# Second cross attention with eight biased exponentials a tile on ACT, a later load of the last experts' weights, and new orders of work

## The reference

```python
q = (x @ W_q).reshape(b, n, HEADS, DIM_HEAD)          # 8 heads of 64
k = (context @ W_k).reshape(b, j, HEADS, DIM_HEAD)    # 64 keys
v = (context @ W_v).reshape(b, j, HEADS, DIM_HEAD)
sim = jnp.einsum('bihd,bjhd->bhij', q, k) * scale     # scale = 1/8
sim = jnp.where(mask[:, None, None, :], sim, max_neg)
attn = jax.nn.softmax(sim, axis=-1)
out = jnp.einsum('bhij,bjhd->bihd', attn, v).reshape(b, n, INNER)
return out @ W_o + b_o
```

## Time and profile before

| | us |
|---|---|
| median of 3 runs | 253.36 (253.21 to 253.58) |
| the profiled execution | 253.86 |
| its span, first to last instruction | 252.1 |
| PE busy | 231.0 |
| DVE busy | 172.7 |
| ACT busy | 142.3 |
| POOL busy | 78.9 |

### The profile page before, as it was taken

How to read it: one execution, slowest core, us unless ns; L and a number is a source line. 1 busy time by engine, 2 the same in 40 slices (tenths; PEclk the granted TensorE clock), 3 DMA queues, 4 the chain that set the end, 5 groups by cost and what they waited for, 6 DMA issues and landing times.

```text
span 252.1 us, 5538 instructions
## 1 busy us (share of the span) xinstructions
PE 231.0 (92%) x2018; PEld 157.2 (62%) x2018; DVE 172.7 (68%) x574; ACT 142.3 (56%) x297; POOL 78.9 (31%) x137
## 2 busy tenths in 40 slices
PE   8997899878999999999997886899798999999995
PEld 8646577653544766565674543497677575579765
DVE  4472899855858823745236999778655888778995
ACT  0746698953244768765764366675565635434360
POOL 4898900010110565448583131182411000000000
PEclk9999999999999999999999999999999999999999
DMA  4888970494000000000000000000000000000002
GB/s 133 179 184 246 299 178 3 144 314 136 4 0 0 3 3 0 1 0 3 0 1 0 3 1 3 0 3 5 1 3 1 3 0 0 0 4 0 0 3 83
DMA packets 22343, 12.23 MB, mean 49 GB/s; under 512 B 11320, under 2 KB 21309, under 8 KB 22317
## 3 DMA queue, kind: packets, MB, share of 16 engines
q1 hardware_dynamic: 21277, 11.53, 16.7%
q0 software_dynamic: 80, 0.20, 0.8%
q10 hardware_dynamic: 960, 0.16, 0.4%
HBM read 8.74 MB, written 3.15 MB: 47 GB/s over the span
## 4 chain that ended last, share of the span: by engine, by line
PE 36%; DVE 12%; POOL 2%; ACT 2%; issue 1%; DVEq 0%
PE bank L1047 11%; PE bank L1059 10%; PE bank L930 2%; PE bank L1032 2%; PE bank L911 2%; DVE stats L1805 2%; PE bank L969 2%; PE bank L898 1%; PE bank L1005 1%; PE bank L1019 1%; DVE sm L2029 1%; DVE XN L2005 1%; DVE XN L1827 1%; PE bank L1086 1%; POOL Es L537 1%
## 5 line engine op out<-in xcount | busy, mean ns | idle before, releaser
L448 POOL TENSOR_TENSOR rs<-rs,halves 128x4 f32<-128x4 f32 x14 | 14.3, 1022 | 79.7 <-DVE rs L1820 63.8
L524 POOL TENSOR_TENSOR X<-X,att 128x128 f32<-128x128 f32 x72 | 30.6, 462 | 13.1 <-ACT att L1512 13.1
L1047 PE MATMUL bank<-XT,Wb 128*128 128x512 f32 x64 | 29.6, 597 | 0.0
L1980 DVE SCALAR_TENSOR_TENSOR att<-bank,cols,att 128x512 f32<-128x512 f32 x18 | 13.5, 750 | 22.6 <-ACT att L1501 16.6
L1059 PE MATMUL bank<-Wb,att 128*128 128x128 f32 x224 | 27.4, 278 | 0.0
L1059 PEld LDWEIGHTS bank<-Wb,att 128*128 128x128 f32 x224 | 25.9, 192 | 1.5 <-issue 0.8
L1552 ACT ACTIVATE att<-bank 128x512 f32<-128x512 f32 x32 | 18.0, 601 | 8.4 <-PE bank L1047 8.1
L1512 ACT ACTIVATE att<-bank,comb 128x128 f32<-128x128 f32 x72 | 20.2, 380 | 4.1 <-PE bank L930 4.0
L930 PEld LDWEIGHTS bank<-W2a,att 128*128 128x128 f32 x144 | 18.2, 191 | 6.3 <-issue 4.3
L1501 ACT ACTIVATE att<-bank,cols 128x512 f32<-128x512 f32 x18 | 12.6, 697 | 12.8 <-DVE att L1980 7.4
L1560 ACT ACTIVATE big<-bank 128x512 f32<-128x512 f32 x14 | 8.4, 597 | 18.9 <-PE bank L1059 18.9
(11 more groups left out here) (229 smaller groups left out, 469.3 us busy)
## 6 DMA issues: line engine op xcount, KB each, us to landing
o_scratch<-big SPq DMA_DIRECT2D x2, 512.0 KB, 4.0
Wb<-in_L_ffn_W SPq DMA_DIRECT2D x1, 1024.0 KB, 5.3
Wb<-in_L_ffn_W SPq DMA_DIRECT2D x8, 128.0 KB, 5.0
X<-in_x SPq DMA_DIRECT2D x2, 256.0 KB, 3.2
k_scratch<-QKVT SPq DMA_DIRECT2D x1, 512.0 KB, 3.9
q_scratch<-QKVT SPq DMA_DIRECT2D x1, 512.0 KB, 5.1
Wb<-k_scratch SPq DMA_DIRECT2D x1, 512.0 KB, 4.6
v_scratch<-QKVT SPq DMA_DIRECT2D x1, 512.0 KB, 7.0
```

The costliest lines, as they stand in the source:

```text
L448: nc.gpsimd.tensor_tensor(rs[:, 0, cut], rs[:, 1, cut], halves[:, :], ALU.pow).then_inc(l_root[h], 1)
L524: nc.gpsimd.tensor_tensor(X[:, h * HT + t, :], X[:, h * HT + t, :], part0[:, i % 2, t, :], ALU.add).then_inc(f_acc, 1)
L1047: mm(bank[i % 4][:, :], W1b[:, e, f * P:(f + 1) * P], XT[:, half(h)], start=True, stop=True).then_inc(m_up, 1)
```

## The change

The second cross attention no longer subtracts the maximum on DVE. DVE writes the negated maximum (`negative_max1`); ACT scales the queries as it copies them, takes one exponential for each of the eight heads straight from PSUM with the negated maximum as a bias for each partition, and writes each head's sum with it; DVE takes the reciprocal (`inverse_sums1`). The scores' banks are free, for `scores1(t + 2)` and for the next transposes, once the exponentials are through (c_exp instead of c_sub). W1b and W2b are issued behind the second half of `o_scratch` instead of the first. The lists of PE, ACT, DVE and POOL are reordered in many places; the diff below keeps the functions and the moves that the text names.

```diff
@@ sync
-                if h == 0:
+                if h == 1:
                     sp.wait_ge(a_scores, NU)
                     sp.wait_ge(v2_psum, 2)
                     sp.dma_start(W1b, w["L1_ffn_W1"].rearrange("e d f -> d e f")).then_inc(ld_f1, 16)
...
@@ gpsimd, list
             weigh_probs(0)
+            add_bias(0)
+            add_bias(1)
             weigh_probs(1)
             weigh_probs(2)
-            add_bias(0)
-            add_bias(1)
...
             weigh_probs(6)
+            root(6, 0)
             weigh_probs(7)
-            root(6, 0)
@@ tensor
                 if n == 5 and h == 0:
-                    pe.wait_ge(c_sub, NT - 1)
+                    pe.wait_ge(c_exp, NT - 1)
...
                 if t >= 2:
-                    pe.wait_ge(c_sub, t - 1)
+                    pe.wait_ge(c_exp, t - 1)
@@ tensor, list
+            columns()
             product(0, 0)
-            columns()
...
+            keys_values1(0)
             weigh_values(6)
...
-            keys_values1(0)
             keys_values1(1)
             keys_values1(2)
+            keys_values1(3)
             transpose_xn(1, 0, 7)
-            keys_values1(3)
+            keep_busy(4, 2)
+            keep_busy(4, 3)
             cross0_q(0)
+            cross0_scores(0)
             keep_busy(4, 2)
-            cross0_scores(0)
-            keep_busy(4, 3)
+            keys_values1(4)
             outputs_by_token(1)
             sums_by_token(1)
-            keep_busy(4, 2)
...
             scores1(2)
             transpose_xn(4, 1, 6)
+            transpose_probs1(0)
             queries1(1, 0)
-            transpose_probs1(0)
             queries1(1, 1)
             queries1(1, 2)
             queries1(1, 3)
+            transpose_probs1(1)
+            weigh_values1(0)
             scores1(3)
-            weigh_values1(0)
-            scores1(4)
-            transpose_probs1(1)
             project_out(0)
             weigh_values1(1)
-            scores1(5)
+            scores1(4)
             transpose_probs1(2)
             project_out(1)
             weigh_values1(2)
+            scores1(5)
             transpose_probs1(3)
...
@@ scalar
             def queries1(h, i):
                 act.wait_ge(c_q[h], i + 1)
-                AF(Q1T[:, i, half(h)], bank[4 + 2 * h + i % 2][:, :], ACT.Copy).then_inc(c_qc[h], 1)
+                AF(Q1T[:, i, half(h)], bank[4 + 2 * h + i % 2][:, :], ACT.Copy, scale=XATTN1_SCALE).then_inc(c_qc[h], 1)
 
             def exponentials1(t):
-                act.wait_ge(c_sub, t + 1)
-                AF(Es[:, t % 3, :], Es[:, t % 3, :], ACT.Exp, scale=XATTN1_SCALE).then_inc(c_exp, 1)
+                act.wait_ge(c_max, t + 1)
+                if t >= 3:
+                    act.wait_ge(c_tr, t - 2)
+                for g in range(H1):
+                    h2, a = g // NHP, g % NHP
+                    last = AF(Es[:, t % 3, g * S:(g + 1) * S], bank[2 * (t % 2) + h2][:, a * S:(a + 1) * S], ACT.Exp,
+                              bias=sm[:, t, 0, g:g + 1], accum_out=sm[:, t, 1, g:g + 1])
+                last.then_inc(c_exp, 1)
@@ scalar, list
+            bias_rows()
             projection()
             copy_xt(0, 0, 0)
-            bias_rows()
             copy_xt(0, 1, 1)
             columns()
             project(0, 0)
             project(1, 0)
             project(0, 2)
-            project(1, 2)
             context(0)
             context(1)
+            ssm_operands()
+            project(1, 2)
...
+            value_blocks(0)
             exponentials(0)
-            value_blocks(0)
...
             exponentials1(0)
+            exponentials1(1)
             copy_xt(4, 1, 6)
+            exponentials1(2)
             queries1(1, 0)
+            queries1(1, 1)
             copy_probs1(0)
-            queries1(1, 1)
-            exponentials1(1)
             queries1(1, 2)
             queries1(1, 3)
-            exponentials1(2)
...
             copy_probs1(3)
+            exponentials1(5)
             copy_values1(3)
-            exponentials1(5)
             exponentials1(6)
@@ vector
-            def subtract_max1(t):
+            def negative_max1(t):
                 dve.wait_ge(c_scores, t + 1)
                 s = twin[t % 2][:, :, 0:2 * P].rearrange("p h (a s) -> p h a s", s=S)
-                then(V.tensor_reduce(sm[:, t, 0, :].rearrange("p (h a) -> p h a", h=2), s, AX.X, ALU.max))
-                if t >= 3:
-                    dve.wait_ge(c_tr, t - 2)
-                V.tensor_tensor(Es[:, t % 3, :].rearrange("p (h a s) -> p h a s", h=2, s=S), s,
-                                sm[:, t, 0, :].rearrange("p (h a) -> p h a", h=2).unsqueeze(3).broadcast_to([P, 2, NHP, S]),
-                                ALU.subtract).then_inc(c_sub, 1)
-
-            def probs1(t):
-
+                V.tensor_reduce(sm[:, t, 0, :].rearrange("p (h a) -> p h a", h=2), s, AX.X, ALU.max, negate=True
+                                ).then_inc(c_max, 1)
+
+            def inverse_sums1(t):
                 dve.wait_ge(c_exp, t + 1)
-                e = Es[:, t % 3, :].rearrange("p (a s) -> p a s", s=S)
-                then(V.tensor_reduce(sm[:, t, 1, :], e, AX.X, ALU.add))
                 V.reciprocal(sm[:, t, 2, :], sm[:, t, 1, :]).then_inc(c_sum, 1)
@@ vector, list
             row_max(10)
+            row_max(11)
             subtract_max(10)
-            row_max(11)
             subtract_max(11)
+            mask_row()
...
-            mask_row()
             gate0(1, 8)
...
-            subtract_max1(0)
+            negative_max1(0)
+            negative_max1(1)
             ln_apply(4, 1)
-            probs1(0)
-            subtract_max1(1)
-            subtract_max1(2)
-            probs1(1)
...
+            inverse_sums1(0)
+            inverse_sums1(1)
+            negative_max1(2)
+            negative_max1(3)
+            inverse_sums1(2)
+            inverse_sums1(3)
             add1(0)
-            probs1(3)
+            negative_max1(4)
+            inverse_sums1(4)
             add1(1)
...
+            inverse_sums1(5)
+            inverse_sums1(6)
+            negative_max1(7)
+            ln_moments(5, 0)
+            ln_apply(5, 0)
+            inverse_sums1(7)
             add1(4)
-            ln_moments(5, 0)
-            probs1(7)
             add1(5)
-            ln_apply(5, 0)
+            search_bits()
             add1(6)
             add1(7)
             ln_moments(5, 1)
             ln_apply(5, 1)
-            search_bits()
             route()
```

More of the change, by code:

```diff
@@ L1111, in _ @@
             ssm_operands()
+            power(1)
             keys0(0)
+            power(2)
+            values0(0)
             keys0(1)
-            values0(0)
-            power(1)
-            power(2)
+            power(3)
             values0(1)
-            power(3)
             power(4)
             power(5)
+            power(6)
             scores(0)
             scores(1)
-            power(6)
             transpose_values(0)
@@ L1188, in _ @@
             gate_transpose(0)
+            up0_third(0, 2)
             down0(0, 0)
+            down0(0, 1)
             up0_first(0, 3)
-            up0_third(0, 2)
-            down0(0, 1)
+            up0_first(0, 4)
+            down0(0, 2)
             up0_third(0, 3)
-            down0(0, 2)
+            up0_third(0, 4)
             transpose_xn(2, 1, 7)
-            up0_third(0, 4)
             down0(0, 3)
-            up0_first(0, 4)
-            gate(1)
             up0_first(0, 5)
+            down0(0, 4)
             up0_third(0, 5)
-            down0(0, 4)
+            up0_third(0, 6)
             up0_first(0, 6)
-            up0_third(0, 6)
             down0(0, 5)
@@ L1207, in _ @@
             up0_third(0, 7)
-            up0_third(0, 8)
+            gate(1)
             down0(0, 6)
@@ L1212, in _ @@
             up0_first(1, 0)
+            up0_third(0, 8)
             up0_third(1, 0)
@@ L1247, in _ @@
             read_out(0)
+            keys_values1(9)
             transpose_xn(3, 1, 6)
-            keys_values1(9)
+            keys_values1(10)
             inject(1)
             widen(1, 0)
-            keys_values1(10)
+            keys_values1(11)
             widen(1, 1)
+            keys_values1(12)
             widen(1, 2)
-            keys_values1(11)
             read_out(1)
-            keys_values1(12)
             keys_values1(13)
             keys_values1(14)
+            transpose_xn(4, 0, 0)
             keys_values1(15)
-            transpose_xn(4, 0, 0)
             queries1(0, 0)
@@ L1575, in _ @@
             project(0, 2)
-            project(1, 2)
             context(0)
             context(1)
+            ssm_operands()
+            project(1, 2)
+            power(1)
+            power(2)
             keys0(0)
-            ssm_operands()
-            power(1)
             keys0(1)
-            power(2)
+            power(3)
+            power(4)
             widen_keys(0)
             widen_keys(1)
```

(40 more changed lines are left out.)

56 lines of the change are left out of this document (24 added, 32 removed).

## The result

The changed kernel takes 263.95 us (median of 4, 263.15 to 264.69) against 253.47 for the one before beside it: a ratio of 1.036, interval 1.031 to 1.041. 263.1 was forecast. The profiled execution took 263.83, its span is 262.1, 10.0 more than before.

The account below looks back on a forecast made before the run. PE, busy 231.0 of 252.1 us, bounds the kernel; the second cross attention's chain has no single owner. Profiled 253.86 + 9.3 (stage) + 0.4 (rest) = 263.6, less 0.5 to the median: 263.1; range 255.5 to 269.5.

Parts of the forecast that it names:

- three signs by which I wanted to be wrong: Heads under 0.25 us apart, PE's rows longer (clock), or the stage before 154 moving by more than 1.5 us.
- E: ACT time for one tile's eight exponentials with sums in the second cross attention: 0.33 us a head, 2.64 a tile.
- The 0.20 without the sum: ACT time in us for one 64-column head in a row of eight, read from the weighing of expert outputs.
- 8E - 11.8: Change of the second cross attention's length in us, new orders less old ones: +9.3 at 2.64 a tile.
- the layout: Four engines' orders laid out through the second cross attention: new ends at 195.5 us, old at 186.2; equal at E = 1.48.
- rival 2: Second cross attention: short ACTIVATEs overlap deeply, 0.12 us a head, about 252 us; decides below 0.185 a head; chance 0.07.
- Rival 1: Second cross attention: the sum is free or nearly so, +1.0 to +5.0 us, total 254.7 to 258.5; chance 0.17.
- Rival 4, the clock: PE idles over a third of the second cross attention and its clock halves: +5.5 us, near 268; chance 0.10.
- Start and attention: Reordered start +0.5 us (ends -0.5 and +2); first attention: mask_row +0.4, keys_values1(0) -0.2; +0.4 together with the remaining terms.
- First feed-forward, 0: Moves in the first feed-forward, where PE is full, change no bound engine's work: 0, ends -0.5 and +0.5 us.
- Weights later, -0.3: W1b and W2b loading after the second o_scratch round trip: -0.3 us, the weights still there over 100 us early.
- last feed-forward, 0: Moves in the last feed-forward change the work of no bound engine: 0, ends -0.5 and +0.5 us.

Follow-up runs that it names:

- the rest alone: The changed kernel with the second cross attention of the kernel before; its other orders and later weight load remain: 256.75 us, ratio 1.008.
- keys back: The changed kernel with keys_values1(4) moved back on PE behind cross0_values(0) and on ACT behind cross0_copy(0): 261.98 us, ratio 1.029.
- the run above: The kernel before with two biased exponentials a tile, the changed orders from 80 to 155 us and six idle PE products: 253.36 us, ratio 0.992.

## Why the prediction was right, point by point

The total came out, 9.7 of span forecast and 10.0 found, but from terms that missed in both directions: 1.9 too much in the stage, 2.2 too little ahead of it. What was right is that ACT's eight exponentials with their sums cost more than DVE's relief gives; that the number is so near is luck. Two of the three signs by which I wanted to be wrong came: PE's rows got longer, and the stages before 154 moved by 2.5.

- **E.** Mechanism right, size off: the sum as a short instruction of its own, pipelined; 0.09 a head, not the 0.13 taken halfway between 0.06 and 0.19. E = 2.32, not 2.64: 2.6 us too much. The 0.20 without the sum was exact. The Trainium skill (page "ScalarE: Activation LUTs", section "What ACT_TABLE_LOAD costs") prices an ACTIVATE with one pointer operand and 64 columns, as an estimate, at 186 + 93 + 53 = 332 ns; the trace has 339. Back to back it gives 0.24, the trace 0.20.
- **8E - 11.8.** With the measured E it gives +6.8; the trace has +7.4. That is one point, and the slope isn't borne out. Without the sums E is 1.6 and the stage should have been 5.8 shorter; it was 1.6. With two exponentials, E = 0.83, it was still 3.6 longer than before, where the layout had the new order ahead of the old one below 1.48. Both runs also have DVE's sums back, which the layout leaves out, and a low clock, so how far the layout itself is off there stays open. With that falls the price of rival 2 (252) and its point of decision at 0.185 a head. (Rival 1's upper end is 258.8 by this sum, not 258.5.)
- **Rival 4, the clock.** It happened, but not at its price. I charged five waits on products, +5.5 in the stage; the low stretch ended at about 167, ahead of the first value copy (171.2), and held or low the stage takes 37. Nor did PE idle for over a third of the stage: 29.16 of 38 us were busy. The clock cost elsewhere: 1.4 at 74 to 79, and 0.95 of the 1.8 at the start.
- **Start and attention, +0.4 in all with the rest.** The term that failed most: 2.2 by the last row maximum, and 2.5 by the first maximum of the cross attention, over the 1.5 that I had named as proof against me. At the start I priced when the query load is issued (0.3 later; it went 0.5 earlier) and not when it lands, which was 1.4 later, and no clock. In all seven profiles with the new start the clock is low somewhere between 20 and 32 us and the first row maximum is at 29.1 to 29.9; in all seven with the old start it is 1.00 there and the maximum at 27.5 to 27.7. In three of the seven (the changed kernel, the rest alone, keys back) the scores wait for the query load; in the other four, where the clock is low by 24, they start at 28.1 to 28.8 behind PE's own products. Which of the moved calls opens the gaps, and whether the late value store slows the query load, wasn't separated.
- **First feed-forward, 0.** It gains 1.0 to 1.3: 75.5 or 75.6 in every trace read with the old order, 74.3 to 74.6 in every one with the new. I had called PE full there and looked no further.
- **Weights later, -0.3; last feed-forward, 0.** The first can't be seen: last row maximum to first silu is 31.7 in the rest alone and 31.8 before. The second holds: 66.8 from the last value copy to the end in both.

## What to carry to other kernels

Moving work from one engine to another is to be priced at the receiving engine, instruction by instruction: eight short ACTIVATEs with sums cost 2.32 us where one wide one cost 0.63, and DVE's 1.37 saved a tile could not pay for it. An order of work is good for one set of durations: the same list was worth 8 us in the traces with eight exponentials and cost 1.5 with two. Where PE has gaps, look at the granted clock of several executions, not of one, and give PE some work that is due anyway, or idle products, in the gap: with orders worth 1.3 us, that turned 254 to 259 us into 252.2.

## What the runs showed of the hardware

A sum written out by an ACTIVATE is a record of its own, ACTIVATION_READ_ACCUMULATOR, 233 ns long, of which back to back only 90 are added.

PE's clock goes between 1.00 (2.4 GHz) and 0.50 (1.2 GHz), and products then take close to twice as long (L734 1.91 instead of 1.06). The same program can go either way: 56 executions of the kernel before had a mean clock of 0.999 or 1.00 nineteen times and took 253.07 to 253.85; the other 37, at 0.973 to 0.993, took 254.15 to 258.92. The profiled one was of the first kind, which is why its clock row was all nines. From 48 to 52 us PE is busy 2.52 of 4 in the kernel before, whose clock held, and in the run above, whose clock fell. The Trainium skill (page "TensorE: Matmul & The Clock Gate", section "What's actually happening") calls the low clock the default, which activity lifts, and says that what watches the activity runs freely and does not start with the kernel; the pairs of rows with the same gaps and different clocks agree with it, and no run here shows why an execution falls on one side.
